# A layer kernel (causal attention, then routed experts): another order of steps in each attention slot, and one subtraction moved from VectorE to GpSimd

## The chip, the cores and the metric

The kernel runs on one core of a Trainium2 chip. The metric is the device time of one execution in microseconds (us), lower is better. The engines are TensorE (PE; PEld is its weight load), VectorE (DVE), ScalarE (ACT), GpSimd (POOL) and SyncE (SP), which here only issues DMAs. Each runs its own queue in order; they meet through semaphores alone.

## What is computed

The input x is (16, 512, 128) in float32: 16 batches of 512 tokens, width 128.

```python
x = x + attn(layernorm(x), W_qkv, W_out)     # 16 heads of size 8, causal softmax
x = x + ffn(layernorm(x), ...)
# attn: qkv = einsum('bsd,ndh->bnsh', x, W_qkv); softmax(q k^T / sqrt(8) + mask) v
#       out.reshape(B, -1, S); einsum('bds,nhd->bsd', out, W_out)
# ffn:  probs = softmax(xf @ Wr + br); the top 2 of 8 experts for each token
#       h = gelu(xf @ Wi + bi) * sigmoid(xf @ Wg + bg);  r = xf + h @ Wo + bo
#       y = normalise(r) * gamma + beta;  out = the two experts' y, by their weights
```

## The kernel before, in words

**Two stages.** The attention works through 64 groups (16 batches of 4 groups, 4 heads in each), one after the other. Then 71 blocks of 256 rows, sorted by expert, go through the experts. A last short block adds the two expert rows of each token. The change is in the attention, which takes the first 765 us or so of the profile.

**A slot.** Slot s is the stretch of program in which group s is finished. The table `SLOT` has four strings of tokens, for s mod 4, each token a step. `schedule()` turns them into one list, `ORDER`, and every engine's code walks that same list and issues what belongs to it. So the table sets the order within each engine's queue; between engines only semaphores count. `AHEAD` gives how many groups ahead of s a token works, `BATCH_OF` how many batches ahead. The last slots have strings of their own (`LAST_SLOTS`), and some steps of the last batches run between expert blocks (`GUESTS`).

**The tokens of a group:**

- `A0` to `A5` and `a0` to `a5`, three groups ahead: the six maxima steps. `A` is the first PSUM bank of a step, `a` the second bank and the mask matmuls (L864, L869, tile `sa`); on VectorE `a` is the reduction to the row maxima (L1291). `sa` has two buffers: `A(k)` on TensorE waits until the reduction of step k-2 is over.
- `mT mE mW mR`, two groups ahead: the maxima are transposed on TensorE (L968), copied by VectorE (L1299), stored by SP (L669) and loaded into `q_stack` by SP (L673). `B0` of that group waits until they have landed.
- `B0` to `B11`, one group ahead: the score steps on TensorE (L884, tile `st`, two buffers), their exponentials on ScalarE (L1100), and the causal mask on GpSimd (L801). `B(t)` on TensorE waits for the exponential of t-2.
- `PV0` to `PV3`, of group s: probabilities times values (L897). `OT` and `RC` on VectorE (L1325, L1330) transpose the result and take reciprocals; `ON` scales on GpSimd (L809, L814) and SP stores it (L680).
- `SR`, four groups ahead: SP loads `q_stack` and `k_pad` (L600, L603; five DMAs), which `A0` waits for.

**The tokens of a batch,** once in four slots: `ln rs1 xn xT Q Ql K Kl ST V` make q, k and v two batches ahead (v one ahead); `ln`, `Ql` and `Kl` are VectorE's, `rs1` is GpSimd's, `xn` ScalarE's, `ST` is SP's store of q and k. `XL` and `AR` load x and the attention result; `out` adds them on GpSimd (L311); `ln2 rs2 zn zT LG` are the second layer norm and the router's logits; `LGa Ra Rb Rc Rd Re Rf` are the router on VectorE, chains of small operations on 128x32 elements; `EX` and `CM` are its exponential and its counting matmuls; `S0` to `S7` are GpSimd's indirect DMAs that scatter the rows (L316).

**The tokens `W` and `WS`,** in slots 14 to 29 (`FIRST_SPLIT` is 14), one per slot: an expert weight matrix is split in two parts. ScalarE writes the high part (L1092), VectorE takes the rest by subtraction (L1319), SP stores the high part (L688).

`ONCE` adds single steps to a slot. `SU3` in slot 5 is `constants(3)` on GpSimd: a memset and three selects over 32x1024 (L778, L781).

Of the kernel before, what the change touches and what calls it, by code (L numbers as in the profile page):

```python
# [5 lines left out]
def attention_and_routed_experts(nc, x, w_qkv, w_out, wr, br, wi, bi, wg, bg, wo, bo, gamma, beta, out,  # L6
# [5 lines left out]
    F32, F32R, BF16, I32 = mybir.dt.float32, mybir.dt.float32r, mybir.dt.bfloat16, mybir.dt.int32  # L12
    ALU, ACT, AX = mybir.AluOpType, mybir.ActivationFunctionType, mybir.AxisListType

    B, S, D = x.shape
# [17 lines left out]
    with ctx:  # L33
# [8 lines left out]
        def sem(name):  # L42
# [175 lines left out]


        SLOT = {  # L220
# [4 lines left out]
        }  # L225
        AHEAD = {"SR": 4, "A": 3, "a": 3, "mT": 2, "mE": 2, "mW": 2, "mR": 2, "B": 1, "PV": 0, "OT": 0, "RC": 0, "ON": 0}
        BATCH_OF = {"ln": 2, "rs1": 2, "xn": 2, "xT": 2, "Q": 2, "Ql": 2, "K": 2, "Kl": 2, "ST": 2, "V": 1, "XL": 0,
                    "AR": -1, "out": -1, "ln2": -1, "rs2": -1, "zn": -1, "zT": -1, "LG": -1, "LGa": -1,
                    "Ra": -1, "EX": -1, "Rb": -1, "Rc": -1, "Rd": -2, "CM": -2, "Re": -2, "Rf": -2, "S": -2,
                    "WC": 0, "TAa": -3, "TAb": -3, "WH": 0, "WO": 0, "GBa": 0, "GBb": 0, "GBc": 0, "GBd": 0, "XG": 0, "E": 0}  # L230
        FIRST = "ln rs1 xn xT Q Ql K Kl ST SR0 SR1 SR2 SR3"

        ONCE = {-1: "WL8", 1: "SU0", 2: "SU1", 4: "SU2", 5: "SU3", 6: "WL0", 7: "WL1", 8: "WL2", 9: "WL3", 10: "WL4",
# [4 lines left out]
            -6: SLOT[2] + " WH0 WH1",  # L238
            -5: SLOT[3] + " WH2 WH3",
            -4: SLOT[0] + " WH4 WH5",  # L240
# [3 lines left out]
        }  # L244
        GUESTS = {
# [485 lines left out]
        def _(pool):  # L731
# [54 lines left out]
            for kind, k, n in ORDER:  # L786
                pool_sequence(pool, kind, k, n)
                if kind == "SU":
                    constants(k)
                elif kind == "rs1":  # L790
                    inverse_deviation(pool, n, var1_done, nmean1_done, rstd1_done, rstd, nmean)
                    if n == 0:
                        pool.memset(v_aug[:, :, :, :, :], 0.0).then_inc(v_zero, 1)
                        pool.wait_ge(v_zero, 1)
                        pool.memset(v_aug[:, :, :, :, HD:HD + 1], 1.0).then_inc(v_zero, 1)
                elif kind == "B":
                    third, j = k // G, HEAD_OF[k % G]
                    pool.wait_ge(exp_done, NB_ * n + k + 1)
                    off, w = ((PT_OFF[0], 1), (PT_OFF[1], 1), (PT_OFF[3], 2))[third]
                    blk = probs[:, n % 2, j, off:off + w * P].rearrange("p (a q) -> p a q", q=P)  # L800
                    pool.affine_select(out=blk, in_=blk, compare_op=ALU.is_ge, fill=0.0, base=0,  # L801
                                       pattern=[[0, w], [1, P]], channel_multiplier=-1).then_inc(masked, 1)
                elif kind == "ON":
                    g = n % NG
                    by_m = o_t[:, :, :].rearrange("p (m u) c -> p u c m", u=2)
                    pool.wait_ge(rden_done, n + 1)
                    if n == 0:
                        pool.wait_ge(wsum_done, 1)
                    pool.tensor_tensor(r_scale[:, :, :], r_den[:, :, :], wsum[:, g, :, :], ALU.mult)\  # L809
                        .then_inc(rscale_done, 1)  # L810
                    pool.wait_ge(rscale_done, n + 1)
                    if n >= 2:
                        pool.wait_ge(on_stored[n % 2], 16 * (n // 2))
                    pool.tensor_tensor(o_n[:, n % 2, :, :, :], by_m[:, :, 0:HD, :],  # L814
                                       r_scale[:, :, :].unsqueeze(2).broadcast_to([P, 2, HD, HD]),
                                       ALU.mult).then_inc(on_done, 1)
# [296 lines left out]
        def _(dve):  # L1113
# [155 lines left out]
            for kind, k, n in ORDER:  # L1269
# [10 lines left out]
                elif kind in ("Ql", "Kl"):  # L1280
                    hi, lo, scale = (q_hi, q_lo, SCALE) if kind == "Ql" else (k_hi, k_lo, 1.0)
                    if n == 0:
                        dve.wait_ge(rows_filled, 32)
                    dve.wait_ge(hi_done, 2 * n + (1 if kind == "Ql" else 2))
                    V.scalar_tensor_tensor(lo[:, :], misc[:, :], scale, hi[:, :].bitcast(F32),
                                           ALU.mult, ALU.subtract).then_inc(lo_done, 1)
                elif kind == "a":
                    i, heads = A_STEPS[k]
                    dve.wait_ge(sa_written, NA * n + k + 1)
                    scores = sa[:, k % 2, :, :].rearrange("p b (e k) -> p (b e) k", e=len(heads) // 2)  # L1290
                    V.tensor_reduce(neg_max[:, n % 2, heads[0]:heads[-1] + 1, i], scores[:, :, 0:(i + 1) * P],  # L1291
                                    AX.X, ALU.max, negate=True).then_inc(sa_read, 1)
                elif kind == "mE":
                    dve.wait_ge(maxT_written, n + 1)
                    if n + 1 < GROUPS_ALL:
                        dve.wait_ge(sa_written, NA * (n + 1) + 3)
                    if n >= 2:
                        dve.wait_ge(max_stored, 16 * (n - 1))
                    V.tensor_copy(neg_maxT[:, n % 2, :], sa[0:G * NT, 0, 1, S - P:S]).then_inc(maxT_done, 1)  # L1299
                elif kind == "E":  # L1300
                    if k > 0:
                        load_expert(k, k)
                    low_x(k, k)
                elif kind == "WC":
                    load_expert(0, 0)
                    copy_weights(0, 0)
                elif kind == "TAa":
                    early_counts(n)
                elif kind == "TAb":
                    early_blocks()  # L1310
                elif kind == "BU":
                    dve.wait_ge(misc_written, misc_use("BU", n))
                    V.tensor_scalar(b_up[:, 0, :], misc[:, 0:E * FC], 1.0, None, ALU.mult)
                    V.tensor_scalar(b_up[:, 1, :], misc[:, E * FC:2 * E * FC], 0.5, None, ALU.mult).then_inc(b_up_done, 1)
                elif kind == "W":
                    m, e = k // E, k % E
                    part_ = w_lo[m][:, e * F:(e + 1) * F]
                    dve.wait_ge(w_hi_done, k + 1)
                    V.tensor_tensor(part_, part_.bitcast(F32), high[:, k % 2, :].bitcast(F32), ALU.subtract)\  # L1319
                        .then_inc(w_lo_done, 1)  # L1320
                elif kind == "OT":
                    dve.wait_ge(pv_written, n + 1)
                    if n > 0:
                        dve.wait_ge(on_done, n)
                    V.transpose(o_t[:, :, :].rearrange("p m c -> p (m c)"), pv[:, :]).then_inc(pv_read, 1)  # L1325
                elif kind == "RC":
                    dve.wait_ge(pv_read, n + 1)
                    if n > 0:
                        dve.wait_ge(rscale_done, n)
                    V.reciprocal(r_den[:, :, :], o_t[:, :, :].rearrange("p (m u) c -> p u c m", u=2)  # L1330
                                 [:, :, HD, :]).then_inc(rden_done, 1)
# [71 lines left out]
```

## Time and profile before

| | |
|---|---|
| median of 3 runs | 1189.0 us (1186.06 to 1190.85) |
| the profiled execution, its own time | 1187.28 us |
| its span, first to last instruction | 1185.2 us |
| PE / PEld busy | 1084.1 us (91%) / 816.9 us (69%) |
| DVE busy | 986.8 us (83%) |
| ACT busy | 802.0 us (68%) |
| POOL busy | 751.6 us (63%) |

The busy share of TensorE is to be read with care: matmuls are pipelined, and the duration shown for one reaches from its issue to its modelled end, so a wait of some tenths of a microsecond can lie inside a matmul's duration. The distance from one start to the next says more, and the idle time of the weight load (PEld) shows waits that the matmul rows hide. On VectorE, too, an operation's shown duration overlaps the next one by about 0.1 us, so a step is taken here from its start to the next start.

### The profile page before, as it was taken

The numbers are of one execution on the slowest core, as the hardware profiler recorded it, in microseconds if no ns is written. First come the engines' busy times: TensorE is split into PE (matmuls) and PEld (weight loads), VectorE is DVE, ScalarE is ACT, GpSimd is POOL, SyncE is SP. The second block draws the span as 40 slices with busy tenths as digits, with TensorE's granted clock in tenths as the row PEclk, the third lists the DMA queues.
The fourth block names the chain that finished last, engine by engine and source line by source line (L and its number), as shares of the span: only waits on it lengthen the run. The fifth ranks groups of instructions, "written<-read, shape, count | busy, mean of one in ns | idle before, by whom it ended". The sixth has DMA issues, their size and how long they took to land. (4 is left out here: it accounts for less than half of the span.)

```text
span 1185.2 us, 27238 instructions
## 1 busy us (share of the span) xinstructions
PE 1084.1 (91%) x8520; PEld 816.9 (69%) x8520; DVE 986.8 (83%) x2743; ACT 802.0 (68%) x1806; POOL 751.6 (63%) x1361
## 2 busy tenths in 40 slices
PE   2899999999999999999999999899999999999920
PEld 1565666666656666666666666589999999999910
DVE  4766788888888888888888788589899999999959
ACT  1465666766766766766666666788888888888810
POOL 2257475765756766766766756648778777777740
PEclk9999899999999999999999999999999999999965
DMA  5224365444344444344344343742213211111148
GB/s 144 91 81 131 99 185 167 129 142 152 114 149 153 113 139 124 90 149 129 96 139 129 93 133 94 214 115 58 61 59 97 61 54 55 53 55 55 33 144 303
DMA packets 142877, 135.74 MB, mean 115 GB/s; under 512 B 72360, under 2 KB 96944, under 8 KB 142736
## 3 DMA queue, kind: packets, MB, share of 16 engines
q1 hardware_dynamic: 131792, 111.98, 31.9%
q0 software_dynamic: 8640, 17.84, 4.5%
q10 hardware_dynamic: 2304, 4.20, 0.9%
q8 instruction: 70, 1.15, 0.4%
q14 instruction: 71, 0.58, 0.2%
HBM read 75.33 MB, written 58.62 MB: 113 GB/s over the span
## 5 line engine op out<-in xcount | busy, mean ns | idle before, releaser
L1100 ACT ACTIVATE probs<-st 128x384 f32<-128x384 f32 (+1 forms) x768 | 389.9, 525 | 179.0 <-PE st L884 168.3
L1291 DVE TENSOR_REDUCE neg_max<-sa 128x2 fp32r<-128x1024 f32 (+3 forms) x384 | 392.8, 1034 | 118.6 <-PE sa L869 117.8
L801 POOL TENSOR_SCALAR_AFFINE_SELECT probs<-probs 128x128 f32<-128x128 f32 (+1 forms) x768 | 248.2, 336 | 231.7 <-ACT probs L1100 224.1
L884 PE MATMUL st<-q_stack,k_pad 128*128 128x256 f32 (+2 forms) x1024 | 335.8, 369 | 10.6 <-ACT probs L1100 7.6
L864 PE MATMUL sa<-k_pad,q_stack 128*128 128x256 f32 (+2 forms) x1024 | 327.2, 362 | 19.6 <-DMA k_pad<-k_scratch 11.3
L864 PEld LDWEIGHTS sa<-k_pad,q_stack 128*128 128x128 f32 x1024 | 176.6, 190 | 114.0 <-issue 70.9
L884 PEld LDWEIGHTS st<-q_stack,k_pad 128*128 128x128 f32 x1024 | 176.0, 190 | 46.8 <-ACT probs L1100 30.0
L827 POOL DMA_INDIRECT y_scratch<-z,to_row x142 | 172.6, 1216 | 35.5 <-issue 35.5
L932 PE MATMUL up<-xt_hi,w_cur 128*128 128x256 f32 x568 | 166.2, 293 | 1.3 <-ACT hid L1026 0.7
L897 PE MATMUL pv<-probs,v_aug 128*32 128x512 f32 (+3 forms) x2048 | 166.4, 443 | 0.0
L933 PE MATMUL up<-xt_lo,w_cur 128*128 128x256 f32 x568 | 160.6, 283 | 0.0
L934 PE MATMUL up<-xt_hi,w_cur 128*128 128x256 f32 x568 | 160.0, 282 | 0.0
L316 POOL DMA_INDIRECT rows_scratch<-xn,dest x128 | 130.9, 1023 | 23.5 <-issue 23.4
L948 PE MATMUL y_ps<-wo_sb,hid 128*128 x1136 | 139.7, 276 | 0.0
L948 PEld LDWEIGHTS y_ps<-wo_sb,hid 128*128 128x128 f32 x1136 | 133.0, 192 | 0.3
L869 PE MATMUL sa<-maskneg,identb 128*128 128x128 bf16 (+1 forms) x768 | 124.6, 244 | 0.0
L1029 ACT ACTIVATE gate<-up,b_cur 128x256 f32<-128x256 f32 x284 | 123.0, 506 | 0.0
L1026 ACT ACTIVATE hid<-up,b_cur 128x256 f32<-128x256 f32 x284 | 120.7, 489 | 1.5 <-PE up L934 1.5
L1135 DVE SCALAR_TENSOR_TENSOR hid<-gate,hid 128x512 f32<-128x512 f32 x142 | 95.4, 688 | 21.4 <-ACT gate L1029 21.3
L821 POOL TENSOR_TENSOR inv_dev<-inv_dev,minus_half 128x2 f32<-128x2 f32 x71 | 79.4, 1119 | 51.7 <-DVE inv_dev L1171 51.0
L932 PEld LDWEIGHTS up<-xt_hi,w_cur 128*128 128x128 f32 x568 | 108.1, 190 | 2.6 <-issue 2.5
L933 PEld LDWEIGHTS up<-xt_lo,w_cur 128*128 128x128 f32 x568 | 108.3, 191 | 0.0
(176 smaller groups left out, 1438.6 us busy)
## 6 DMA issues: line engine op xcount, KB each, us to landing
q_stack<-q_scratch SPq DMA_DIRECT2D x64, 256.0 KB, 2.7
k_pad<-k_scratch SPq DMA_DIRECT2D x256, 64.0 KB, 2.4
xg<-rows_scratch SPq DMA_DIRECT2D x71, 130.0 KB, 2.1
q_scratch<-q_hi SPq DMA_DIRECT2D x16, 512.0 KB, 3.1
k_scratch<-k_hi SPq DMA_DIRECT2D x16, 512.0 KB, 2.9
y<-y_scratch SPq DMA_DIRECT2D x16, 512.0 KB, 5.6
q_scratch<-q_lo SPq DMA_DIRECT2D x17, 256.0 KB, 3.2
k_scratch<-k_lo SPq DMA_DIRECT2D x17, 256.0 KB, 3.1
```

What stands on the lines that cost most here:

```text
L316: pool.indirect_dma_start(rows_d, bass.IndirectOffsetOnAxis(dest[:, n % 2, k:k + 1], 0), xn2[:, n % 2, k % NT, :], None).then_inc(rows_sto ...
L801: pool.affine_select(out=blk, in_=blk, compare_op=ALU.is_ge, fill=0.0, base=0, pattern=[[0, w], [1, P]], channel_multiplier=-1).then_inc(m ...
L827: pool.indirect_dma_start(y2_d, bass.IndirectOffsetOnAxis(to_row[:, u, h:h + 1], 0), z[:, u % NR, h, :], None).then_inc(scattered[u % NR], 16)
L864: nc.tensor.matmul(sa[:, s % 2, bank, h * 2 * P:h * 2 * P + width], q_stack[:, g, i * P:(i + 1) * P], k_pad[:, G * g + heads[bank * each + ...
L884: last = nc.tensor.matmul(st[:, t % 2, at:at + w], k_pad[:, G * g + j, kk * P:(kk + 1) * P], q_stack[:, g, S - w:S], start=True, stop=True)
L897: last = nc.tensor.matmul(pv[R * j:R * j + R, kk * P:S], v_aug[:, b % 2, kk, G * g + j, :], probs[:, n % 2, j, PT_OFF[kk]:PT_OFF[kk] + w], ...
L932: nc.tensor.matmul(dst, lo, xt_hi[:, b2, :], start=True, stop=False)
L933: nc.tensor.matmul(dst, hi, xt_lo[:, b2, :], start=False, stop=False)
L934: last = nc.tensor.matmul(dst, hi, xt_hi[:, b2, :], start=False, stop=True)
L948: last = nc.tensor.matmul(y_ps[:, h, :], hid[:, u % 2, c, h * P:(h + 1) * P], wo_sb[:, bass.ds(e * (FC * D) + c * D, D)], start=False, sto ...
L1100: nc.scalar.activation(probs[:, n % 2, j, lo:lo + w], st[:, k % 2, at:at + w], ACT.Exp).then_inc(exp_done, 1)
L1291: V.tensor_reduce(neg_max[:, n % 2, heads[0]:heads[-1] + 1, i], scores[:, :, 0:(i + 1) * P], AX.X, ALU.max, negate=True).then_inc(sa_read, 1)
```

## The change

It has four parts. The four strings of `SLOT` are rewritten; `Rd` moves from slot 0 to slot 3 of the slot cycle before (its batch offset goes from -2 to -1), `Re` and `Rf` move from slot 0 to slot 1, `ln` from slot 2 to slot 1, `S0` to `S6` stand in slot 2 (before: `S0` to `S2` in slot 1, `S3` and `S4` in slot 2, `S5` to `S7` in slot 3), and `XL` moves from slot 0 to the slot 3 before it. `Re Rf` are added to the string of slot 61, and `out` and `S7` change places in `GUESTS`. The subtraction of `W` is issued by GpSimd. The work itself is the same.

```diff
         SLOT = {
-            0: "A0 B0 a0 Rd B1 PV0 A1 B2 a1 B3 CM mT mE A2 W B4 mW SR a2 B5 A3 B6 a3 B7 A4 B8 Re Rf PV1 PV2 PV3 a4 OT B9 mR AR XL A5 B10 RC WS a5 B11 ON",
-            1: "SR A0 B0 a0 B1 PV0 A1 B2 out a1 B3 mT mE A2 W S0 B4 mW a2 ln2 B5 V A3 rs2 B6 a3 B7 A4 S1 B8 zn PV1 PV2 PV3 a4 OT B9 mR S2 A5 B10 RC WS a5 B11 ON",
...
+            0: "B0 A0 B1 a0 PV0 B2 A1 B3 a1 mT B4 A2 B5 mE a2 CM mW A3 SR B6 a3 W mR AR PV1 PV2 PV3 B7 A4 OT a4 B8 B9 A5 a5 B10 RC WS ON B11",
+            1: "A0 Re a0 A1 out a1 B0 Rf B1 PV0 mT SR B2 B3 A2 mE a2 ln2 A3 B4 a3 W rs2 mW mR B5 B6 V B7 A4 a4 B8 PV1 PV2 zn PV3 B9 ln A5 OT a5 RC B10 B11 WS ON",
+            2: "rs1 A0 S0 a0 B0 S1 S2 zT S3 SR A1 B1 B2 a1 PV0 mT B3 B4 LG B5 A2 xn mE B6 S4 a2 mW A3 B7 a3 W PV1 PV2 S5 LGa PV3 B8 OT mR Ra B9 xT A4 a4 RC WS ON B10 B11 A5 S6 a5 EX",
+            3: "B0 B1 SR A0 a0 A1 B2 Rb a1 PV0 mT PV1 B3 A2 mE B4 a2 Q Ql mW B5 S7 A3 B6 Rc a3 W B7 A4 K XL B8 Rd PV2 PV3 B9 a4 OT B10 A5 Kl B11 RC mR ST WS ON a5",
         }
...
+                elif kind == "W":
+                    m, e = k // E, k % E
+                    part_ = w_lo[m][:, e * F:(e + 1) * F]
+                    pool.wait_ge(w_hi_done, k + 1)
+                    pool.tensor_tensor(part_, part_.bitcast(F32), high[:, k % 2, :].bitcast(F32), ALU.subtract)\
+                        .then_inc(w_lo_done, 1)
```

The rest of the diff removes the same five lines from VectorE's code. Three places show what the queues become.

VectorE in slot 1, from `ln2` on (L1291 is a maxima reduction, `stats`, `mv`, `rstd` and `nmean` are a layer norm's statistics). Before:

```order
L479 BN_STATS stats<-x_all 128x6 x4
L482 BN_AGGR mv<-stats 128x2 x4
L484 TENSOR_SCALAR rstd<-mv 128x4
L485 TENSOR_SCALAR nmean<-mv 128x4
L1291 TENSOR_REDUCE neg_max<-sa 128x2
L1291 TENSOR_REDUCE neg_max<-sa 128x4
L1325 STREAM_TRANSPOSE o_t<-pv 128x512
L1330 RECIPROCAL r_den<-o_t 128x16
L1291 TENSOR_REDUCE neg_max<-sa 128x4
```

Now:

```order
L476 BN_STATS stats<-x_all 128x6 x4
L479 BN_AGGR mv<-stats 128x2 x4
L481 TENSOR_SCALAR rstd<-mv 128x4
L482 TENSOR_SCALAR nmean<-mv 128x4
L1294 TENSOR_REDUCE neg_max<-sa 128x2
L1294 TENSOR_REDUCE neg_max<-sa 128x4
L476 BN_STATS stats<-x_row 128x6 x4
L479 BN_AGGR mv<-stats 128x2 x4
L481 TENSOR_SCALAR rstd<-mv 128x4
L482 TENSOR_SCALAR nmean<-mv 128x4
L1322 STREAM_TRANSPOSE o_t<-pv 128x512
L1294 TENSOR_REDUCE neg_max<-sa 128x4
```

Behind `ln2` there stands a second set of statistics, `ln`, between the reductions of steps 4 and 5, ahead of `OT`; before, `ln` stood in slot 2 between the reductions of steps 0 and 1.

TensorE at the end of slot 0 and the start of slot 1 (`sa` with `k_pad` is `A` or `a`, with `maskneg` the mask, `st` is `B`). Before:

```order
L884 MATMUL st<-q_stack,k_pad 128x256 x2
L864 MATMUL sa<-k_pad,q_stack 128x256 x2
L884 MATMUL st<-q_stack,k_pad 128x256 x2
L864 MATMUL sa<-k_pad,q_stack 128x256 x2
L869 MATMUL sa<-maskneg,identb 128x2x128 x2
L884 MATMUL st<-q_stack,k_pad 128x256 x2
L864 MATMUL sa<-k_pad,q_stack 128x512
L884 MATMUL st<-q_stack,k_pad 128x512
L864 MATMUL sa<-k_pad,q_stack 128x512
L869 MATMUL sa<-maskneg,identb 128x128 x2
L884 MATMUL st<-q_stack,k_pad 128x512
```

Now:

```order
L867 MATMUL sa<-k_pad,q_stack 128x256 x4
L872 MATMUL sa<-maskneg,identb 128x2x128 x2
L887 MATMUL st<-q_stack,k_pad 128x256 x4
L867 MATMUL sa<-k_pad,q_stack 128x256 x4
L872 MATMUL sa<-maskneg,identb 128x2x128 x2
L887 MATMUL st<-q_stack,k_pad 128x256 x4
L867 MATMUL sa<-k_pad,q_stack 128x512 x2
L872 MATMUL sa<-maskneg,identb 128x128 x2
L867 MATMUL sa<-k_pad,q_stack 128x512 x2
L872 MATMUL sa<-maskneg,identb 128x128 x2
```

The score steps that stood between the maxima steps are now in pairs behind them, and the first two maxima steps of slot 1 follow each other with nothing between.

GpSimd in slot 2 (AFFINE_SELECT is the mask of a `B`, the DMA is an `S`, `rstd` and `nmean` are `rs1`). Before, from the middle of the slot's first masks to its end:

```order
L801 AFFINE_SELECT probs<-probs 128x128 x2
L442 TENSOR_TENSOR rstd<-rstd,minus_half 128x4
L445 TENSOR_TENSOR nmean<-nmean,rstd 128x4
L316 DMA rows_scratch<-xn,dest 69376x130
L801 AFFINE_SELECT probs<-probs 128x128 x4
L801 AFFINE_SELECT probs<-probs 128x256 x4
L809 TENSOR_TENSOR r_scale<-r_den,wsum 128x16
L814 TENSOR_TENSOR o_n<-o_t,r_scale 128x128
```

Now, from the slot's start:

```order
L439 TENSOR_TENSOR rstd<-rstd,minus_half 128x4
L442 TENSOR_TENSOR nmean<-nmean,rstd 128x4
L313 DMA rows_scratch<-xn,dest 69376x130
L804 AFFINE_SELECT probs<-probs 128x128
L313 DMA rows_scratch<-xn,dest 69376x130 x3
L804 AFFINE_SELECT probs<-probs 128x128 x6
L313 DMA rows_scratch<-xn,dest 69376x130
L804 AFFINE_SELECT probs<-probs 128x128
L797 TENSOR_TENSOR wg_lo<-wg_lo,high 128x512
L313 DMA rows_scratch<-xn,dest 69376x130
```

`rs1` opens the slot, and three scatters follow in a row behind the first mask; the subtraction of `W` comes in as a TENSOR_TENSOR on GpSimd.

## Rows read from the trace of the kernel before

**Rows 1.** The profile page: busy time, share and instructions of each engine.

```profile
PE 1084.1 (91%) x8520; PEld 816.9 (69%) x8520; DVE 986.8 (83%) x2743; ACT 802.0 (68%) x1806; POOL 751.6 (63%) x1361
```

**Rows 2.** Windows of two batches: length, busy PE, PEld, DVE, ACT, POOL; then clock.

```profile
330.00:376.30 46.30, 44.47 (x343) 28.47 (x342) 39.49 (x89) 31.43 (x66) 30.13 (x70) 1.00 0.44 135
466.40:510.80 44.40, 44.17 (x344) 28.70 (x342) 37.28 (x85) 29.91 (x62) 29.55 (x70) 1.00 0.37 108
```

**Rows 3.** Windows of one batch's slots 0, 1, 2, 3, same columns.

```profile
466.40:476.50 10.10, 10.06 (x84) 6.26 (x82) 9.06 (x23) 6.29 (x12) 4.72 (x16) 1.00 0.44 144
476.50:487.70 11.20, 11.01 (x87) 7.24 (x86) 8.76 (x20) 8.00 (x17) 8.82 (x19) 1.00 0.45 115
487.70:498.70 11.00, 11.00 (x92) 7.63 (x90) 8.96 (x23) 8.15 (x17) 8.74 (x21) 1.00 0.25 73
498.70:510.80 12.10, 12.09 (x87) 7.57 (x86) 10.50 (x22) 7.46 (x16) 7.27 (x17) 1.00 0.34 102
```

**Rows 4.** Weight-load waits, 100 to 700 us: releaser, total us, times, longest.

```profile
PEld st L884 <- ACT probs L1100: 20.4, 61, 1.6
PEld sa L864 <- DVE neg_max L1291: 13.2, 28, 2.7
```

**Rows 5.** Timeline of TensorE in slot 1: start us, us, line, tiles, shapes.

```profile
479.24 0.40 PE L884 MATMUL st<-q_stack,k_pad 128*128 128x512 f32 x1
479.48 0.39 PE L864 MATMUL sa<-k_pad,q_stack 128*128 128x512 f32 x1
...
479.80 0.48 PE L884 MATMUL st<-q_stack,k_pad 128*128 128x512 f32 x1
```

**Rows 6.** Timeline of VectorE in three slots, the same columns.

```profile
480.03 1.23 DVE L1291 TENSOR_REDUCE neg_max<-sa 128x2 fp32r<-128x1024 f32 x1 [1.07 <-PE sa L869]
481.17 0.27 DVE L1299 COPY neg_maxT<-sa 16x128 f32<-16x128 f32 x1
...
482.24 0.85 DVE L479 BATCH_NORM_STATS2 stats<-x_all 128x6 f32<-128x128 f32 x4
...
483.80 0.94 DVE L1291 TENSOR_REDUCE neg_max<-sa 128x2 fp32r<-128x768 f32 x1
...
506.95 0.67 DVE L385 TENSOR_TENSOR tmp<-pr,pm 128x32 f32<-128x32 f32 x1
...
508.78 1.23 DVE L1291 TENSOR_REDUCE neg_max<-sa 128x4 fp32r<-128x1024 f32 x1
...
513.10 0.18 DVE L385 TENSOR_TENSOR tmp<-pr,pm 128x32 f32<-128x32 f32 x1
...
514.11 1.23 DVE L1291 TENSOR_REDUCE neg_max<-sa 128x2 fp32r<-128x1024 f32 x1
515.47 0.28 DVE L1299 COPY neg_maxT<-sa 16x128 f32<-16x128 f32 x1
...
517.40 0.14 DVE L421 TENSOR_TENSOR sm<-pm 128x4 f32<-128x4 f32 x1
...
518.77 0.17 DVE L437 CAST dest<-dest_f 128x8 int32<-128x8 f32 x1
```

**Rows 7.** One line's instructions: min/median/max ns, first and last start.

```profile
L1319 DVE TENSOR_TENSOR wg_lo<-wg_lo,high x8: 668/681/956, 312.0 to 391.9; 128x512 fp32r<-128x512 f32 x8
```

**Rows 8.** Groups of GpSimd, 100 to 700 us: count, busy us and mean ns.

```profile
L311 POOL TENSOR_TENSOR x_all<-x_all,att 128x512 f32<-128x512 f32 x13 | 16.6, 1280 | 0.0
```

**Rows 9.** Windows of slots 5 and 6, of 6's start, columns as above.

```profile
106.50:134.90 28.40, 24.68 (x176) 16.10 (x175) 17.34 (x42) 16.32 (x34) 17.96 (x43) 0.88 0.28 80
121.70:126.50 4.80, 4.80 (x19) 2.17 (x18) 2.18 (x8) 2.28 (x4) 1.82 (x6) 0.51 0.26 73
```

**Rows 10.** Timeline of GpSimd in slot 5.

```profile
110.28 3.54 POOL L781 TENSOR_SCALAR_AFFINE_SELECT b_sel<-b_sel 32x1024 bf16<-32x1024 bf16 x3
```

**Rows 11.** Waits of VectorE, 104 to 136 us.

```profile
DVE stats L479 <- POOL x_all L311: 3.9, 1, 3.9
```

**Rows 12.** Timeline of TensorE at the first step of a slot 1.

```profile
521.30 0.50 PE L864 MATMUL sa<-k_pad,q_stack 128*128 128x512 f32 x1 [0.37 <-DMA k_pad<-k_scratch]
```

More of the change, by code:

```diff
@@ L220, in attention_and_routed_experts @@
         SLOT = {
[4 rows of a table removed]
[4 rows of a table added]
         }
         AHEAD = {"SR": 4, "A": 3, "a": 3, "mT": 2, "mE": 2, "mW": 2, "mR": 2, "B": 1, "PV": 0, "OT": 0, "RC": 0, "ON": 0}
[L227 to L230, printed above, removed]
+        BATCH_OF = {'ln': 2, 'rs1': 2, 'xn': 2, 'xT': 2, 'Q': 2, 'Ql': 2, 'K': 2, 'Kl': 2, 'ST': 2, 'V': 1, 'XL': 1, 'AR': -1, 'out': -1, 'ln2': -1, 'rs2': -1, 'zn': -1, 'zT': -1, 'LG': -1, 'LGa': -1, 'Ra': -1, 'EX': -1, 'Rb': -1, 'Rc': -1, 'Rd': -1, 'CM': -2, 'Re': -2, 'Rf': -2, 'S': -2, 'WC': 0, 'TAa': -3, 'TAb': -3, 'WH': 0, 'WO': 0, 'GBa': 0, 'GBb': 0, 'GBc': 0, 'GBd': 0, 'XG': 0, 'E': 0}
         FIRST = "ln rs1 xn xT Q Ql K Kl ST SR0 SR1 SR2 SR3"
@@ L1314, in _ @@
                     V.tensor_scalar(b_up[:, 1, :], misc[:, E * FC:2 * E * FC], 0.5, None, ALU.mult).then_inc(b_up_done, 1)
[L1315 to L1320, printed above, removed]
                 elif kind == "OT":
```

6 rows, old and new, of tables (GUESTS, LAST_SLOTS, SLOT) are left out of this document.

## The prediction

> **What bounds the kernel now.** I read the page first. TensorE is busy for 1084 of 1185 us, its clock in the attention is granted in full [rows 1, 2]; so time can be saved only where TensorE waits, and lost wherever another queue makes it wait longer. The change touches the attention alone, so the next view is windows over it. A batch of four slots takes 44.4 us late in the attention, and 46.3 us where the `W` steps run [rows 2]. In one undisturbed batch the slots 0 to 3 take 10.1, 11.2, 11.0 and 12.1 us [rows 3], and VectorE is busy for 9.1, 8.8, 9.0 and 10.5 us of them. It is the engine nearest to TensorE: its 37.3 of 44.4 us leave 7 us in a batch. ScalarE (29.9 us) and GpSimd (29.6 us) have twice that.
>
> How much can an order win? The matmul rows hide short waits, the weight load shows them: over 600 us it waits 20.4 us for exponentials and 13.2 us for reductions [rows 4]. That is 33.6 us in 600, or 2.5 us in a batch of 44.4. Some of it only looks like waiting, since a long matmul was still running. So 2.5 us a batch is the ceiling of what the new strings can bring, and I expect a part of it.
>
> **The W step.** The change takes one subtraction per slot off VectorE, in slots 14 to 29. It takes 0.68 us there in the median and 0.96 at most [rows 7]. The four batches with it are 1.9 us longer than one without (46.3 against 44.4, [rows 2]), 7.6 us in all. The high part that ScalarE writes stays, so not all comes back: I take 6 us. On GpSimd the same size, two inputs and 512 columns, takes 1.28 us [rows 8]. That is hidden: GpSimd is busy for 30 of 46 us in such a batch [rows 2], and what it delays are masks which `PV` reads a slot later. If the cover fails, the price is at most 16 times 1.28, 20 us; at best the gain is the 7.6 us.
>
> While GpSimd works, some of VectorE's operations wait. One of 32 columns with two SBUF inputs took 0.67 us beside a scatter on GpSimd and 0.18 us in the next slot, where none ran (506.95 and 513.10, [rows 6]). The Trainium skill, "SBUF — State Buffer", section "Who interferes with whom", has the rule: the two engines share a port pair under an exclusive lock, held for the whole instruction, and a VectorE operation with two SBUF inputs needs it. The trace agrees. By that rule the moved subtraction can block the router's chains, which have such operations; in the new slot 3 it stands right among `Rc` and `Rd`, one slot in four. Four meetings at 1.28 us would make 5 us, and the forecast would be 1178 instead of 1173; I leave it out of the sum, because VectorE is not waited for at every one of them.
>
> **The stall of slot 5.** GpSimd makes constants there, three selects that take 3.54 us [rows 10]. `out` stands behind them and behind three masks, and VectorE waits 3.9 us for it before `ln2` [rows 11]; everything late in that slot and the next follows. Slots 5 and 6 take 28.4 us [rows 9], against 11.2 and 11.0 later [rows 3], 6.2 us more. In the new string `out` stands ahead of all masks of its slot and `ln2` is asked for later, behind `Re`, two reductions and `Rf`. A part of the 6.2 us is the clock: after the stall TensorE is granted less than in the other batches, 0.88 as a mean over both slots and 0.51 at the start of slot 6 [rows 9], which is the lower of its two levels, 1.2 for 2.4 GHz. If the stall goes, so does that. I take 4 of the 6.2 us, with 0 and 6 as the ends.
>
> **The slots.** Here I walk the new strings with durations of the trace, start to start. TensorE: a score step 0.24 us, a bank with its masks 0.32 us [rows 5]. VectorE: a reduction of 1024 columns 1.14 us (480.03 to 481.17); `ln2` or `ln` 1.56 us (482.24 to 483.80); `Rc` 1.83 us (506.95 to 508.78); `Rd` 1.01 us (513.10 to 514.11); `Re` and `Rf` 1.55 us (517.40 to 518.77 and 0.17), all in [rows 6].
>
> The load of VectorE becomes uneven. From its busy time in rows 3: slot 0 gives up `Rd`, `Re` and `Rf`, 9.1 - 2.6 = 6.5 us; slot 1 takes in `Re`, `Rf` and `ln`, 8.8 + 3.1 = 11.9; slot 2 gives up `ln`, 9.0 - 1.6 = 7.4; slot 3 takes in `Rd`, 10.5 + 1.0 = 11.5. So slots 1 and 3 ask VectorE for more than TensorE's slots of 11.2 and 12.1 leave comfortably, and it must catch up in slots 0 and 2. TensorE may run only two maxima steps ahead of it.
>
> *Slot 1*, counted from TensorE's `A0`. VectorE, whose later times follow from the durations above, comes out of the light slot 0 with nothing behind. It is done with reduction 0 at 2.1, 1 at 3.3, `Rf` 4.3, the copy 4.5, reduction 2 at 5.4, `ln2` 6.9, reduction 3 at 7.8, 4 at 8.9, `ln` 10.4, `OT` 11.1, reduction 5 at 11.7. TensorE asks for reduction 2 at 6.1 (`A4`) and for 3 at 8.9 (`A5`): no wait. `B11` needs the exponential of `B9`, which stands behind `zn` on ScalarE; `rs2` on GpSimd ends 1.3 us after `ln2`, `zn` at about 10.0, the exponential at 10.5. `B11` would be issued at 10.1, so 0.5 us are lost, as much as the order before loses near that place. Slot 1 takes 11.1 us.
>
> *Slot 2*: `A1` asks for reduction 5 at 1.2 us into the slot, that is 12.2, half a microsecond after it is done; with VectorE light from there on, no wait above 0.2 us. GpSimd falls far behind: `rs1`, then a scatter of 1.0 us, a mask and three more scatters; its masks 0 to 3 are done about 9 us into the slot, and `PV0` asks for them 2 us into the next. Slot 2 takes 11.05 us.
>
> *Slot 3*: `Rc` in front of reduction 3 and `Rd` behind it put that reduction's end at 9.7 us into the slot; `A5` asks at 10.2. Reduction 4 ends at 11.8, and `A0` of slot 0 asks at about 11.8; reduction 5 ends at 13.8, and `A1` of slot 0 asks at 13.9. All three fit by 0.1 to 0.5 us. Before, `K` and `Q` pile up with `Rc` at these places; I get 11.55 instead of 12.1 us.
>
> *Slot 0*: it cannot be shorter than about 10.2 us, whatever VectorE does. SP issues `SR` behind `mW`, behind the copy of the maxima, and the next slot's `A0` waits for its transfers: before, the start at 521.30 waited for `k_pad` [rows 12], 5.5 us after the end of the copy of 515.47 [rows 6]. In the new string the copy again comes some 4.8 us into the slot.
>
> Together 11.1 + 11.05 + 11.55 + 10.2 = 43.9 against 44.4 [rows 2]: 0.45 us a batch, 6 us for some 13 whole batches. The ends are minus 33 us (the ceiling above, 2.5 times 13) and the rival below.
>
> **Edits at nothing.** `Re Rf` in slot 61 put 1.55 us on VectorE, which has no reductions left there; if `OT` is late by it, the price is 1.5 us. `XL` is asked for later than it is issued in both. `out` and `S7` swapped in `GUESTS` lie beside expert blocks.
>
> **The sum.** 6 + 4 + 6 = 16 us. The profiled execution took 1187.3 us and would take 1171; the median, 1189.0, stands 1.7 us above it, and that gives **1173 us**.
>
> **The rivals.**
> - *The strings bring nothing* (0.22): each wait removed comes back in another place, and only `W` and slot 5 count. 1189 - 10 = 1179 us. For it: TensorE already waits little [rows 4]. Against it: slot 3's 12.1 us.
> - *The strings bring most of the ceiling* (0.12): pairs of score steps hide the reductions, and 2 us go per batch. 1189 - 10 - 26 = 1153 us. Against it: the transfers of `SR` hold slot 0.
> - *VectorE overrun, slower* (0.15): in slots 1 and 3 its 11.9 and 11.5 us are not worked through without gaps. If it idles 1 us in each, waiting for banks, as it does before its reduction at 480.03 (1.07 us, [rows 6]), slot 1 takes 12.9 and slot 3 12.5 us, against the 11.1 and 12.1 of before, plus 1.8 and 0.4. The light slots catch up the rest. That is 2.2 us a batch, 29 us; less 10 it makes 1208 us. The point from which it decides is the lead at `A1` of slots 2 and 0: 0.5 and 0.1 us. Once VectorE is later than that, every further tenth is TensorE's.
> - *The change does nothing that can be measured* (0.08): the gains of `W` and slot 5 are paid for by SP or GpSimd, whose queues are now denser: `ON` of slot 2 stands behind six scatters' time and holds back `SR` and `mW` on SP, and `B0` opens slots 0 and 3 and waits for `mR`. 0.7 us a batch gives 1189 us.
>
> **How the numbers follow.** My forecast has 0.43, with a range of its own of 1165 to 1181. What a measurement of this kernel can tell from no change is about 0.5%, 6 us. Faster by more: 0.43, most of the second case and all of the third, less some spread: 0.68. Within: 0.16. Slower by more: 0.16. The range leaves out the far half of the large gain and most of the overrun: 1156 to 1194 us.
>
> **What would show it.** Right: batches 4 to 7 as long as the others; slot 3 below 11.8 us; the 3.9 us wait for `out` gone; slot 0 still ended by `k_pad`. Wrong: the weight load's wait for reductions rises above 13.2 us, first at `A1` of slots 2 and 0; or `st` waits longer for `q_stack` at `B0` of slots 0 and 3.

## The result, and the profile after

The changed kernel takes 1182.0 us in the median of 17 runs (1179.0 to 1184.9), the one before 1189.0 us (1185.9 to 1191.7). The ratio is 0.9945, with a 95% interval of 0.9936 to 0.9955: faster by 0.55%, about 7 us. The forecast was 16 us. The profiled execution took 1184.2 us, its span is 1182.1 us.

The profile page of the changed kernel, part 1, answers to [rows 1]:

```profile
PE 1070.2 (91%) x8520; PEld 813.2 (69%) x8520; DVE 978.5 (83%) x2727; ACT 791.3 (67%) x1806; POOL 760.2 (64%) x1377
```

Windows of the changed kernel: first a batch with `W` steps and a quiet one [rows 2], then the slots 0 to 3 of the quiet one [rows 3]. Columns as there: stretch and length, then busy time of PE, PEld, DVE, ACT and POOL.

```profile
331.50:378.00 46.50, 43.42 (x344) 28.15 (x342) 38.71 (x86) 31.07 (x67) 34.97 (x75) 1.00 0.45 136
465.50:509.80 44.30, 43.19 (x344) 28.25 (x342) 37.12 (x85) 29.25 (x63) 29.32 (x70) 1.00 0.42 122
```

```profile
465.50:476.30 10.80, 10.11 (x85) 6.46 (x82) 9.48 (x15) 6.09 (x13) 4.60 (x15) 1.00 0.48 153
476.30:487.20 10.90, 10.77 (x86) 7.15 (x87) 10.21 (x34) 7.75 (x17) 6.70 (x17) 1.00 0.37 82
487.20:498.10 10.90, 10.90 (x96) 7.73 (x94) 7.57 (x13) 8.47 (x20) 9.31 (x19) 1.00 0.36 104
498.10:509.80 11.70, 11.41 (x83) 6.92 (x82) 9.87 (x25) 6.93 (x16) 8.71 (x22) 1.00 0.47 145
```

The quiet batch is where the walk of the prediction can be checked. It has 44.3 us for the 44.4 us of before; four batches in a row, slots 32 to 47, take 176.4 us for 177.7, 0.3 us less each. Slot by slot the walk said 10.2, 11.1, 11.05 and 11.55 us; the rows say 10.8, 10.9, 10.9 and 11.7, and the slots 0 of the next batches 11.0, 10.2 and 10.5. VectorE's load is less uneven than forecast: 9.5, 10.2, 7.6 and 9.9 us busy for 6.5, 11.9, 7.4 and 11.5 (its lag carries work from slot 3 into slot 0). The batches with `W` were to lose 1.5 us each by the moved subtraction. The one shown lost nothing, 46.5 us against 46.3. The four of them together, slots 16 to 31, take 182.7 us for 184.7. Four quiet batches also become 1.3 us shorter, so some 0.7 us is left for the subtraction.

Waits of the weight load, 100 to 700 us, against [rows 4]:

```profile
PEld st L887 <- ACT probs L1103: 33.2, 78, 1.5
...
PEld sa L971 <- DVE neg_max L1294: 22.6, 27, 0.8
...
PEld sa L867 <- DVE neg_max L1294: 7.5, 17, 2.5
```

Waiting for exponentials grew from 20.4 to 33.2 us. The wait for reductions moved: `A` waits less (7.5 for 13.2 us), but the transpose of the maxima (L971), which now comes 2 to 3 us into a slot, waits 22.6 us. These waits are not all loss: among TensorE's own waits, those of the matmul rows, none at `mT` is listed. But the forecast's sign of failure, "rises above 13.2 us", is met (30.1 us with both), at `mT` and not at `A1`.

**Slots 5 and 6.** The windows answer to [rows 9], the third being the whole stretch at the lower clock; the timeline of GpSimd answers to [rows 10], the wait of VectorE to [rows 11]. TensorE's two waits stand last:

```profile
107.90:135.70 27.80, 24.16 (x179) 16.51 (x179) 16.59 (x41) 16.75 (x37) 18.20 (x43) 0.88 0.32 82
122.70:126.50 3.80, 3.80 (x14) 2.81 (x13) 2.03 (x4) 1.88 (x4) 2.76 (x7) 0.50 0.21 25
120.80:127.50 6.70, 5.38 (x22) 3.74 (x25) 3.96 (x15) 4.44 (x10) 3.98 (x11) 0.50 0.22 51
```

```profile
106.77 3.09 POOL L804 TENSOR_SCALAR_AFFINE_SELECT probs<-probs 128x128 f32<-128x128 f32 x11
...
112.04 3.54 POOL L778 TENSOR_SCALAR_AFFINE_SELECT b_sel<-b_sel 32x1024 bf16<-32x1024 bf16 x3
115.83 1.27 POOL L308 TENSOR_TENSOR x_all<-x_all,att 128x512 f32<-128x512 f32 x1 [0.25 <-POOL b_sel L778]
```

```profile
DVE stats L476 <- POOL x_all L308: 3.9, 1, 3.9
```

```profile
PE sa L867 <- DVE neg_max L1294: 2.3, 1, 2.3
PE st L887 <- ACT probs L1103: 1.3, 1, 1.3
```

The stall is all there: 27.8 us for 28.4, the same 3.9 us wait, the same clock of 0.50 at the start of slot 6. `out` now stands ahead of its slot's masks, but GpSimd comes to the constants only 3 us into the slot (a memset at 110.95, not shown), because it still works on masks of slot 4 (eleven from 106.77 on), and `out` starts at 115.83, 7.9 us into the slot; before, it was 8.3 (114.76 after 106.5).

**The batches with W.** Three timelines around the end of slot 19: VectorE, GpSimd, TensorE.

```profile
281.82 1.89 DVE L412 SCALAR_TENSOR_TENSOR pr<-oh,pr 128x32 f32<-128x32 f32 x1
...
283.96 0.96 DVE L1294 TENSOR_REDUCE neg_max<-sa 128x2 fp32r<-128x768 f32 x1
...
285.96 1.22 DVE L1294 TENSOR_REDUCE neg_max<-sa 128x4 fp32r<-128x1024 f32 x1
```

```profile
281.10 0.98 POOL L313 DMA_INDIRECT rows_scratch<-xn,dest  x1 [0.16 <-issue]
282.10 0.30 POOL L804 TENSOR_SCALAR_AFFINE_SELECT probs<-probs 128x128 f32<-128x128 f32 x1
282.37 1.28 POOL L797 TENSOR_TENSOR wi_lo<-wi_lo,high 128x512 fp32r<-128x512 f32 x1
```

```profile
284.98 0.50 PE L867 MATMUL sa<-k_pad,q_stack 128*128 128x256 f32 x2 [0.65 <-DVE neg_max L1294]
...
287.32 0.47 PE L867 MATMUL sa<-k_pad,q_stack 128*128 128x512 f32 x1 [0.89 <-DVE neg_max L1294]
```

One operation of `Rc` (L412, 32 columns, two SBUF inputs) took 1.89 us; in the same chain of a quiet batch it takes 0.2. By its row it began while the scatter was still running, and it ended at 283.71, when GpSimd's subtraction (282.37 + 1.28) had ended at 283.65. Reduction 3 (283.96) and reduction 4 (285.96) came late by that much, and TensorE waited for them twice, 0.65 us at `A5` and 0.89 us at the next slot's `A0`.

The subtraction stands in slot 3 four times. In slots 15 and 19 it meets L412, which takes 1.89 us both times; in slots 23 and 27 it meets the first operation of `Rd`, which takes 0.80 and 0.81 us for 0.2. In slot 23 the subtraction ends at 330.39, the operation at 330.45:

```profile
329.65 0.80 DVE L382 TENSOR_TENSOR tmp<-pr,pm 128x32 f32<-128x32 f32 x1
```

```profile
329.11 1.28 POOL L797 TENSOR_TENSOR wg_lo<-wg_lo,high 128x512 fp32r<-128x512 f32 x1
```

Together the four are 4.6 us longer than four times 0.2.

The trace of before has the same thing, and the prediction read it wrongly. The operation of 0.67 us there (506.95 in [rows 6]) did not stand beside a scatter, which had ended at 506.64, but beside masks:

```profile
506.67 0.90 POOL L801 TENSOR_SCALAR_AFFINE_SELECT probs<-probs 128x128 f32<-128x128 f32 x3
```

It ended at 507.62, they at 507.57. Such an operation, 0.62 to 0.68 us long beside masks, opens `Rc` in every batch of the old order from slot 11 to slot 55; in the new order it takes 0.2 us there in the quiet batches.

### The profile page after: what moved, and what is told of

Read it like the earlier page. It is cut to its first block and busy times, and to the rows that moved or that the text cites. A ratio compares the mean times of both kernels' runs of the same rounds, so it can differ in the third digit from the quotient of the medians.

```text
span 1182.1 us, 27238 instructions
## 1 busy us (share of the span) xinstructions
PE 1070.2 (91%) x8520; PEld 813.2 (69%) x8520; DVE 978.5 (83%) x2727; ACT 791.3 (67%) x1806; POOL 760.2 (64%) x1377
## 5 line engine op out<-in xcount | busy, mean ns | idle before, releaser
L1103 ACT ACTIVATE probs<-st 128x384 f32<-128x384 f32 (+1 forms) x768 | 378.5, 524 | 215.8 <-PE st L887 209.2
L804 POOL TENSOR_SCALAR_AFFINE_SELECT probs<-probs 128x128 f32<-128x128 f32 (+1 forms) x768 | 242.3, 333 | 161.1 <-ACT probs L1103 156.4
L887 PE MATMUL st<-q_stack,k_pad 128*128 128x256 f32 (+2 forms) x1024 | 321.5, 378 | 16.5 <-ACT probs L1103 11.3
L867 PE MATMUL sa<-k_pad,q_stack 128*128 128x256 f32 (+2 forms) x1024 | 274.3, 341 | 23.8 <-DMA k_pad<-k_scratch 11.9
L887 PEld LDWEIGHTS st<-q_stack,k_pad 128*128 128x128 f32 x1024 | 168.0, 190 | 91.8 <-ACT probs L1103 46.6
L867 PEld LDWEIGHTS sa<-k_pad,q_stack 128*128 128x128 f32 x1024 | 169.6, 192 | 42.4 <-DMA k_pad<-k_scratch 15.3
L313 POOL DMA_INDIRECT rows_scratch<-xn,dest x128 | 128.0, 1000 | 27.3 <-issue 27.0
L824 POOL TENSOR_TENSOR inv_dev<-inv_dev,minus_half 128x2 f32<-128x2 f32 x71 | 75.8, 1068 | 58.0 <-DVE inv_dev L1174 57.7
```

What stands on the lines that cost most here:

```text
L313: pool.indirect_dma_start(rows_d, bass.IndirectOffsetOnAxis(dest[:, n % 2, k:k + 1], 0), xn2[:, n % 2, k % NT, :], None).then_inc(rows_sto ...
L867: nc.tensor.matmul(sa[:, s % 2, bank, h * 2 * P:h * 2 * P + width], q_stack[:, g, i * P:(i + 1) * P], k_pad[:, G * g + heads[bank * each + ...
L887: last = nc.tensor.matmul(st[:, t % 2, at:at + w], k_pad[:, G * g + j, kk * P:(kk + 1) * P], q_stack[:, g, S - w:S], start=True, stop=True)
L1103: nc.scalar.activation(probs[:, n % 2, j, lo:lo + w], st[:, k % 2, at:at + w], ACT.Exp).then_inc(exp_done, 1)
```

## The experiments

Beside each time stands the ratio to the kernel before, measured on the same chip. The lengths of stretches, from TensorE's first instruction of one slot to that of another, are each from the one profiled execution, which need not be a typical one: that of `after_w_dve` is the slowest of its eleven (1190.4 us), that of `after_su3` the fastest of its five (1172.4 us).

| kernel | median us | ratio (95% interval) | slots 4-7 | slots 16-31 | slots 32-47 |
|---|---|---|---|---|---|
| before | 1187 to 1190 | 1 | 50.3 | 184.7 | 177.7 |
| changed | 1182.0 | 0.9945 (0.9936 to 0.9955) | 49.7 | 182.7 | 176.4 |
| `before_w_pool` | 1184.7 | 0.9981 (0.9969 to 0.9993) | 49.4 | 182.9 | 177.4 |
| `after_w_dve` | 1186.2 | 0.9984 (0.9974 to 0.9994) | 49.9 | 186.3 | 176.3 |
| `after_w_late` | 1176.9 | 0.9907 (0.9893 to 0.9922) | 48.7 | 177.5 | 176.9 |
| `after_su3` | 1175.4 | 0.9902 (0.9887 to 0.9918) | 44.0 | 181.2 | 176.3 |
| `before_su3` | 1181.4 | 0.9939 (0.9917 to 0.9960) | 43.9 | 185.3 | 177.7 |
| `before_both` | 1178.7 | 0.9938 (0.9920 to 0.9956) | 44.2 | 184.4 | 177.4 |
| `both_late` | 1171.2 | 0.9853 (0.9828 to 0.9877) | 44.8 | 176.7 | 176.4 |
| `extra_at_router` | 1176.0 | 0.9894 (0.9872 to 0.9916) | 44.1 | 179.0 | 178.1 |
| `extra_behind_ot` | 1171.4 | 0.9854 (0.9827 to 0.9881) | 45.0 | 177.0 | 176.6 |
| `sr_first` | 1181.6 | 0.9960 (0.9942 to 0.9978) | 44.7 | 182.4 | 179.6 |

The theory under test, the **lock theory**: GpSimd's work on SBUF holds up VectorE's operations with two SBUF inputs, and where the router chain stands next to the subtraction that costs TensorE time. The rivals say that the place does not matter.

**The subtraction alone, in the old strings.**

```diff
                 elif kind == "W":
...
-                    dve.wait_ge(w_hi_done, k + 1)
-                    V.tensor_tensor(part_, part_.bitcast(F32), high[:, k % 2, :].bitcast(F32), ALU.subtract)\
...
+                    pool.wait_ge(w_hi_done, k + 1)
+                    pool.tensor_tensor(part_, part_.bitcast(F32), high[:, k % 2, :].bitcast(F32), ALU.subtract)\
...
```

> The kernel before, with the subtraction of W issued by GpSimd and nothing else changed. Lock theory: the move loses only where GpSimd's subtraction meets a VectorE operation with two SBUF inputs; in the old strings W stands between reductions, which read PSUM, so most of the gain must show here: 4 to 7 us faster than before, and the four batches with W at 44.7 to 45.2 us for 46.2. Rival (the price of W before was ScalarE's copy of 0.62 us, which stays): no gain, within 1.5 us of the kernel before, the batches still at 46 us.

Measured: 0.9981, some 2 us (3.6 by the medians), and 182.9 us for 184.7 over slots 16 to 31. Neither theory had it right. Slot 0 fell from 10.7 us and more to 10.2, as good as quiet; slot 1 rose from 12.0 us to 12.3 (quiet: 11.1). Its rows, GpSimd and ScalarE:

```profile
297.24 1.29 POOL L800 TENSOR_TENSOR wi_lo<-wi_lo,high 128x512 fp32r<-128x512 f32 x1
...
300.22 1.04 POOL L442 TENSOR_TENSOR rstd<-rstd,minus_half 128x4 f32<-128x4 f32 x1
```

```profile
301.66 1.65 ACT L450 ACTIVATE xn<-x_all,nmean,rstd 128x128 f32<-128x128 f32 x4 [2.11 <-POOL nmean L445]
```

`rs2` (L442) needs VectorE's `rstd`, which is ready at 298.87, and starts 1.35 us later, behind the subtraction, a scatter and two masks; `zn` on ScalarE waits 2.11 us for it, where it waited 1.60 us in the kernel before. TensorE, which in the same place waits for an exponential behind `zn`, does so for 1.43 us against 0.92. So the old slot 1 has its own price for the move, GpSimd's queue.

**The new strings alone:** in the changed kernel the subtraction goes back to VectorE (the diff above, reversed).

> The changed kernel, with the subtraction of W back on VectorE. Lock theory: the operation of 1.89 us in the router chain of slot 3 goes back to about 0.3 us, but VectorE has 0.68 us more work in a slot that is already full; the two about cancel, within 2 us of the changed kernel's 1182. Rival (GpSimd's part was free and VectorE's load alone counts): 4 to 8 us slower than the changed kernel, near 1187.

1186.2 us, 4 us slower than the changed kernel: the rival's number, and not the lock theory's. One half of the lock theory's expectation did come: L412 takes 0.22 us at most, and the slots 3 fall back to 11.8 us. What is lost is lost in the slots 2 of the batches with `W`, 12.6 to 13.0 us for 10.9 in three of them and 11.7 in the fourth. TensorE's wait for VectorE in that run (200 to 700 us), and VectorE in slot 22:

```profile
PE misc L462 <- DVE logits L394: 6.0, 4, 1.8
```

```profile
318.08 1.71 DVE L1316 TENSOR_TENSOR wg_lo<-wg_lo,high 128x512 fp32r<-128x512 f32 x1 [0.61 <-ACT high L1089]
319.71 0.18 DVE L394 TENSOR_TENSOR logits<-misc,br_bc 128x32 f32<-128x32 f32 x1
```

The subtraction waits for ScalarE's high part, `LGa` (L394) stands behind it, and TensorE's transposes of `xT` (L462) need the tile `misc` that `LGa` reads: 6.0 us in four waits, in slots 14, 18, 22 and 26. There the subtraction, which also has two SBUF inputs, takes 1.33, 1.01, 1.71 and 1.72 us while GpSimd works on masks beside it; in the other twelve slots it takes 0.68. The hold goes both ways there: the mask that runs at its end takes 0.73 us for 0.29 (319.20 to 319.93 in slot 22). So the rival's number does not show the rival's cause: the load of 0.68 us is only a part of it.

**The subtraction away from the router.**

```diff
-            3: "... A3 B6 Rc a3 W B7 A4 K XL B8 Rd PV2 PV3 B9 a4 OT B10 A5 Kl ...",
+            3: "... A3 B6 Rc a3 B7 A4 K XL B8 Rd PV2 PV3 B9 a4 OT W B10 A5 Kl ...",
```

> The changed kernel, with the token W of slot 3 moved behind OT, where VectorE has reductions, the transpose and the low part of k next to it, none with two SBUF inputs. Lock theory: the long router operation falls to 0.3 us, the waits of TensorE at B10 of slot 3 and at A0 of the next slot 0 go in the four batches: 3 to 7 us faster than the changed kernel, 1175 to 1179. Rival (GpSimd's queue or ScalarE's copy costs the time, wherever it stands): no gain, 1181 to 1183.

1176.9 us, 5 us faster, as the lock theory had it. Slots 16 to 31 take 177.5 us for 182.7, nearly as little as the quiet slots 32 to 47 of the same run (176.9 us): the `W` step is all but free. The window; the line of the long operation (min/median/max); then TensorE's waits for reductions from 200 to 420 us, first in the changed kernel, then here:

```profile
235.70:413.20 177.50, 173.07 (x1366) 112.93 (x1366) 147.92 (x339) 121.86 (x263) 135.76 (x292) 1.00 0.48 147
```

```profile
L412 DVE SCALAR_TENSOR_TENSOR pr<-oh,pr x4: 208/260/324, 276.5 to 410.0; 128x32 f32<-128x32 f32 x4
```

```profile
PE sa L867 <- DVE neg_max L1294: 3.9, 5, 0.9
```

```profile
PE sa L867 <- DVE neg_max L1294: 0.3, 1, 0.3
```

The longest of its times is 324 ns, where the changed kernel has 1890 ns in that window. The waits for reductions fall by 3.6 us of the 5.2. The edit also moves ScalarE's copy, which belongs to the same token, so by itself it does not tell lock from copy; the runs with an additional operation do.

**The constants two slots later.**

```diff
-        ONCE = {..., 5: "SU3", 6: "WL0", 7: "WL1", ...
+        ONCE = {..., 5: "WL1", 6: "WL0", 7: "SU3", ...
```

> The changed kernel, with the constants of SU3 made in slot 7 and not in slot 5 (the load WL1 takes its place). If they are what holds back the addition out and the layer norm behind it: VectorE's wait of 3.9 us goes, TensorE's clock stays full at the start of slot 6, slots 5 and 6 take 22 to 23 us for 27.9, 4 to 5 us faster than the changed kernel, 1177 to 1178. Rival (the stall moves to slot 7 with them): slots 7 and 8 grow by as much, no gain.

1175.4 us, 6.6 us faster by the medians (5 by the ratios). Slots 4 to 7 take 44.0 us for 49.7, slots 5 and 6 22.0 us, and the clock is full throughout; the stall did not move to slot 7 (11.8 us). The window of slots 5 and 6:

```profile
105.70:127.70 22.00, 21.70 (x178) 14.82 (x178) 16.29 (x41) 16.48 (x37) 14.03 (x39) 1.00 0.46 127
```

> The kernel before, with the constants of SU3 made in slot 7 and WL1 in slot 5, nothing else. If the stall of slot 5 is the constants' own and has nothing to do with the new strings, the gain is the one seen in the changed kernel: slots 5 and 6 at 22 to 23 us for 28.4, 5 to 6 us faster than the kernel before, near 1183. If the new strings had a part in it, less than 3 us.

In the old strings the same edit brings 0.6%, 7 us (43.9 us for 50.3 over slots 4 to 7). The stall had nothing to do with the strings, and the strings did nothing against it.

**Both edits,** then an additional GpSimd operation in two places.

> The changed kernel with both edits: W of slot 3 behind OT, and SU3 in slot 7. The two gains lie in different slots (5.0 and 6.6 us alone) and should add: 1170 to 1172. If one of them only uncovers the other's wait, above 1174.

1171.2 us, 10.8 us below the changed kernel; the 5.0 and 6.6 of the single edits add up to within 1 us.

```diff
+                elif kind == "DU":
+                    if n < 12:
+                        if n > 0:
+                            pool.wait_ge(extra_done, n)
+                        source = ident[:, 0:E].unsqueeze(1).broadcast_to([P, 40, E])
+                        pool.tensor_tensor(passed[:, 0:40, :], source, source, ALU.subtract).then_inc(extra_done, 1)
...
+            3: "... B6 Rc a3 DU B7 ...",       # extra_at_router
+            3: "... B9 a4 OT DU W B10 ...",    # extra_behind_ot
```

> The kernel with both edits, and in slot 3 of twelve batches one more GpSimd operation with two SBUF inputs, 320 columns, about 0.8 us by the rows of its neighbours, into a tile that is unused then. It stands where W stood, behind the masks beside the router chain Rc. Lock theory: operations of that chain wait for it, slots 3 and 0 grow by 0.5 to 1 us per batch in all twelve, 5 to 12 us slower than with both edits. Rival (GpSimd's work is free as long as its masks come a slot early): within 2 us.

> The same additional GpSimd operation in the same slots, but behind OT, where VectorE's neighbours have no two SBUF inputs. Lock theory: no cost, within 2 us of the kernel with both edits. Rival (the load on GpSimd's queue counts, not the place): as slow as with the operation at the router.

The same instruction, twelve times: 1176.0 us at the router, 1171.4 behind `OT`, against 1171.2 without it. At the router it costs 0.4 us each, less than the 0.5 to 1 us expected but clear (its lowest time, 1174.3 us, is above the highest of the other two, 1174.0); behind `OT` nothing. VectorE's timeline of slot 39 with it, GpSimd's, TensorE's, and VectorE's of the same slot without it:

```profile
495.65 0.69 DVE L1295 SCALAR_TENSOR_TENSOR q_lo<-misc,q_hi 128x512 fp32r<-128x512 f32 x1 [0.41 <-ACT q_hi L1069]
...
497.23 0.65 DVE L413 SCALAR_TENSOR_TENSOR pr<-oh,pr 128x32 f32<-128x32 f32 x1
...
500.22 1.22 DVE L1301 TENSOR_REDUCE neg_max<-sa 128x4 fp32r<-128x1024 f32 x1
```

```profile
497.51 0.30 POOL L811 TENSOR_SCALAR_AFFINE_SELECT probs<-probs 128x128 f32<-128x128 f32 x1
497.77 0.72 POOL L799 TENSOR_TENSOR passed<-ident 128x320 f32<-128x320 f32 x1
```

```profile
501.59 0.47 PE L874 MATMUL sa<-k_pad,q_stack 128*128 128x512 f32 x1 [0.66 <-DVE neg_max L1301]
```

```profile
491.72 0.69 DVE L1288 SCALAR_TENSOR_TENSOR q_lo<-misc,q_hi 128x512 fp32r<-128x512 f32 x1 [0.41 <-ACT q_hi L1062]
...
493.33 0.21 DVE L412 SCALAR_TENSOR_TENSOR pr<-oh,pr 128x32 f32<-128x32 f32 x1
...
495.78 1.22 DVE L1294 TENSOR_REDUCE neg_max<-sa 128x4 fp32r<-128x1024 f32 x1
```

From the low part of q (L1295, L1288) to reduction 4 the chain takes 4.57 us with and 4.06 without, and 0.44 us of the 0.51 is again the one operation, 0.65 us for 0.21. It ended at 497.88, 0.07 us after the mask (497.51 + 0.30) and 0.6 us before the additional operation: the place decides, but here the operation was not held for the whole 0.72 us. TensorE then waits 0.66 us for a reduction at `A0` of the next slot 0; without the additional operation no wait is listed there. The next slot 0 is 0.5 to 0.7 us longer in these batches (10.75 and 11.63 for 10.24 and 10.91).

**The worth of the strings:** the constants and the subtraction moved in the kernel before.

> The old strings with W on GpSimd and SU3 in slot 7. Against the changed kernel with both edits (1171 us) this is the pure price of the strings. If the walk's 0.45 us a batch is what the strings bring, near 1178 (6 to 8 us above 1171). If the new strings bring nothing once the two edits are in, 1171 to 1173.

1178.7 us. With the two other things out of the way the new strings, with `W` moved in them, are worth 7.5 us by the medians and 10 by the ratios; the walk said 6. Slots 16 to 31 still take 184.4 us there: the slots 1 take 12.3 to 12.6 us, as in `before_w_pool`, and one slot 2 takes 12.7, which I did not trace.

**SR ahead of mW in slot 0.**

```diff
-            0: "... mE a2 CM mW A3 SR B6 a3 W mR AR ...",
+            0: "... mE a2 CM SR mW A3 B6 a3 W mR AR ...",
```

> The changed kernel with both edits, and in slot 0 SR ahead of mW on SP. If the transfers of SR are what ends slot 0, they start about 0.4 us earlier and slot 0 loses up to 0.4 us of its wait in most batches: 2 to 5 us faster than 1171. Rival (SR then waits for the store of k, which lands at about that moment, or the maxima now arrive late for B0 of slot 1): no gain or up to 5 us slower.

A miss by both: 1181.6 us, 10 us (13 by the ratios) slower than with `mW` first. Slot 0 hardly changes; slot 1 takes 11.3 to 13.2 us for 10.6 to 11.2. Who waits on TensorE, 200 to 700 us, first here, then in `both_late`:

```profile
PE st L887 <- DMA q_stack<-max_scratch: 7.0, 10, 1.1
```

```profile
PE st L887 <- DMA q_stack<-max_scratch: 1.1, 3, 0.7
```

The five DMAs of `SR` occupy SP for about 2.2 us, the store and the load of the maxima come later by that, and `B0` of slot 1 waits for them; TensorE's waits for the maxima grow by 5.9 us, of the 10. In one batch of `sr_first` SP issued the loads of `SR` from 509.98 to 512.16, the store of the maxima at 512.26 and their load at 515.19, and TensorE began `B0` at 517.14, after 0.58 us of waiting for that load. In `both_late` the store goes ahead of the five.

## Why the prediction was wrong

**The W step, 6 us.** This failed first. The subtraction takes 1.28 us on GpSimd as forecast, but "That is hidden" was wrong. The price was named, "Four meetings at 1.28 us would make 5 us", and left out of the sum "because VectorE is not waited for at every one of them". Slot 3 was the one slot where the same text gave VectorE a lead of only 0.1 to 0.5 us, so it had to be in the sum. `after_w_late` measures it: 5 us, and the four long operations are together 4.6 us too long. With them out of the way slots 16 to 31 are 7.2 us shorter than before, 1.3 of them the strings', and the other 5.9 are the 6 that the step was to bring. With the named price in the sum the forecast would have been 1178, nearer to 1182 than 1173 was. The Trainium skill, "SBUF — State Buffer", section "Who interferes with whom", has an exclusive lock between GpSimd and such VectorE operations, those with two SBUF inputs, held for the whole instruction. The long operations agree with it, having ended 0.05 or 0.06 us after GpSimd's subtraction; the one beside the additional operation ended 0.6 us before that did. The sentence of the prediction that set the rule beside the trace took masks for a scatter; scatters beside the same chain did no harm (505.87 to 506.84 in the changed kernel, when the chain's operations took 0.18 to 0.27 us). And the 0.68 us on VectorE was not the whole price of leaving the step there: `after_w_dve` shows the subtraction itself held to 1.0 to 1.7 us beside masks.

**The stall of slot 5, 4 us.** Failed. "`out` stands ahead of all masks of its slot": true, and worth about half a microsecond (28.4 to 27.8 us, at a mean clock of 0.88 in both). The stall is the constants' 4.6 us and the masks queued before them, and the prediction gave no time at which GpSimd would come to them. Moving the constants brings 6.6 us with the new strings, the clock with it, and the 6.2 us named as the upper end were the size.

**The slots, 6 us.** Right in size, if somewhat high for the change as made: walked 43.9 us a batch, measured 44.1 (176.4 for four) against 44.4, about 4 us for 13 batches. The whole worth of the strings, from `before_both` and `both_late`, is 7.5 to 10 us, the queue in the old slot 1 with it. Right too: slot 3 below 11.8 us, slot 0 still ended by transfers. Not seen: that `mT` waits for its reduction in the new slots, and that slot 0 varies from 10.2 to 11.0 us. The walk's 1.83 us for `Rc` was also read from a chain with the held operation of 0.67 us in it; in the quiet batch of the new order `Rc` takes 1.44 us (505.61 to 507.05). How much of the strings' gain comes from the masks no longer holding it, no run separates.

**The sum.** 6 + 4 + 6 became 7 us by the medians. The stretches give about 1 for `W`, 1 for the stall and 4 to 5 for the strings; these shares are estimates, since the two profiled executions lie only 3 us apart. The rivals: the overrun of VectorE did not come by itself, but the lead of 0.1 us at `A0` and `A1` of slot 0 was indeed a point at which a stray 1.7 us became TensorE's (0.89 us at `A0` after slot 19). The range, 1156 to 1194, held, but it reached from a gain of 33 us to a loss of 5; the size did not hold.

**Left open:** which GpSimd instruction exactly holds a VectorE operation and for how long; only places were compared.

## What to carry to other kernels

When work is moved to GpSimd, look at what VectorE does beside it at that moment, and not at GpSimd's busy share: behind `OT`, beside PSUM reductions, it was free, beside a chain of small two-input operations it cost 5 us in 1182. Where a step of constants or any other one-time work stands in a tight slot, move it before tuning the order around it; that alone was worth 6.6 us, about as much as the whole change. A walk start to start, with durations from the trace, came within 0.2 us of a 44 us batch, but each lead of a few tenths that it leaves has to be priced with the next disturbance.

## What the runs showed of the hardware

- A VectorE operation of 32 columns with two SBUF inputs, 0.2 us alone, took up to 1.89 us while GpSimd went from a scatter over a mask to a 512-column subtraction without a pause; it ended 0.06 us after the subtraction. Masks alone do it too: 0.67 us for 0.2 in the kernel before, and 1.71 us for 0.68 for a 512-column subtraction on VectorE in `after_w_dve`.
- An additional GpSimd operation of 0.72 us cost 0.4 us each beside such a chain, and nothing measurable beside PSUM reductions and a transpose (1171.4 and 1171.2 us).
- In slot 5 of the changed kernel TensorE waited 2.3 us, worked for 1.2 us, and then its granted clock fell to 0.50, the lower of its two levels, where it stayed for 6.7 us (120.8 to 127.5), a second wait of 1.3 us among them. Without the waits the clock stayed full (1.00 over slots 5 and 6 in `after_su3`). In `after_w_late` TensorE waited as long, but the mean clock of the two slots was 0.94 for 0.88 and they took 26.9 us for 27.8. Of the 5.8 us that the two slots lose against `after_su3`, 3.6 are TensorE's waits; the other 2 or so are the clock's share, an estimate by subtraction.
